# A planner's account of DMA speed in a selective-scan and feed-forward kernel: 220 or 300 KB per microsecond

## The reference

```python
proj = x @ W_in.T; u, gate = split(proj)              # 2 x 2048 channels
u = silu(causal_conv4(u) + conv_b)
dt, B, C = split(u @ Wx.T)                            # 64, 16, 16 columns, each rms-normed
delta = softplus(dt @ Wdt.T + dt_bias)
state = exp(delta * A) * state + delta * u * B        # a scan over 512 steps, 2048 channels x 16 states
y = (sum over the 16 states of state * C + u * D) * silu(gate)
x = layernorm(x + y @ W_out.T)
x = layernorm(x + x @ W.T + b + the low-rank product that a router picks for the row)
```

## Time and profile before

| | |
|---|---|
| runs | 2258.07, 2259.97, 2263.01 us; median 2259.97 |
| span of the profiled execution, first to last instruction | 2257.2 us |
| its own time | not listed apart from the runs; the median run is 2.8 us above this span |
| TensorE, VectorE, ScalarE, GpSimd busy | 91%, 88%, 66%, 81% of the span |
| TensorE clock granted, mean | 0.964 of full speed |
| DMA | 354.84 MB, mean 157 GB/s |

### The profile page before, as it was taken

The page is one execution under the profiler, slowest core; times in us unless marked ns, Lnnn a source line. Parts: engine busy times, 40 slices in busy tenths (PEclk is TensorE's granted clock), DMA queues, the critical chain, the costliest instruction groups (busy, mean ns, idle before and its releaser), DMA issues. The chain is left out here.

```text
span 2257.2 us, 30761 instructions
## 1 busy us (share of the span) xinstructions
PE 2063.3 (91%) x10528; PEld 1562.5 (69%) x10528; DVE 1986.4 (88%) x2398; ACT 1486.3 (66%) x2198; POOL 1824.8 (81%) x786
## 2 busy tenths in 40 slices
PE   8989789889999799799998997989999998897998
PEld 6867577778565478687875555867875556785677
DVE  4447779999999999899999999999999999999943
ACT  4478658787666677666886657676786667756531
POOL 4279899998898889768799997979788998698840
PEclk9989899999999999999999998999999999998999
DMA  4466566665333447655463432475463337443340
GB/s 157 138 223 235 204 221 219 203 205 179 92 118 86 126 132 239 209 193 182 158 199 95 111 96 96 147 264 171 143 203 101 110 96 233 148 144 132 101 143 38
DMA packets 168764, 354.84 MB, mean 157 GB/s; under 512 B 18656, under 2 KB 45408, under 8 KB 168608
## 3 DMA queue, kind: packets, MB, share of 16 engines
q1 hardware_dynamic: 168608, 352.87, 48.6%
HBM read 283.96 MB, written 68.85 MB: 156 GB/s over the span
## 5 line engine op out<-in xcount | busy, mean ns | idle before, releaser
L1563 POOL TENSOR_TENSOR drive<-delta_u,b_bcast 128x2048 f32<-128x2048 f32 (+1 forms) x257 | 1172.5, 4564 | 129.1 <-PE state_t L933 120.6
L1115 DVE TENSOR_TENSOR_SCAN drive<-decay,drive 128x512 f32<-128x512 f32 x1024 | 1190.5, 1203 | 62.0 <-POOL drive L1563 37.9
L1355 ACT ACTIVATE decay<-delta,a_sb 128x512 f32<-128x512 f32 x1024 | 694.7, 688 | 377.9 <-DVE drive L1115 374.6
L933 PEld LDWEIGHTS state_t<-identity,drive 128*128 128x128 f32 x4096 | 492.0, 146 | 311.1 <-DVE drive L1115 141.8
L933 PE MATMUL state_t<-identity,drive 128*128 128x128 f32 x4096 | 591.1, 284 | 119.8 <-DVE drive L1115 95.1
L1123 DVE SCALAR_TENSOR_TENSOR y_acc<-state_t,c_rows,y_acc 128x512 f32<-128x512 f32 x727 | 515.3, 734 | 54.3 <-PE state_t L933 51.7
L964 PE MATMUL bank<-cols_high,w_split 128*128 128x512 f32 (+1 forms) x1240 | 524.4, 423 | 26.6 <-POOL w_split L1588 11.8
L966 PE MATMUL bank<-cols_high,w_split 128*128 128x512 f32 (+1 forms) x1240 | 491.8, 397 | 0.0
L965 PE MATMUL bank<-cols_low,w_split 128*128 128x512 f32 (+1 forms) x1240 | 489.6, 395 | 0.0
L987 PE MATMUL bank<-channels,w_raw 128*128 128x512 f32 x896 | 420.2, 596 | 2.3 <-DVE rows L1177 2.0
L1568 POOL TENSOR_TENSOR y_acc<-y_acc,scaled 128x512 f32<-128x512 f32 x233 | 300.1, 1288 | 102.2 <-ACT scaled L1375 101.9
(11 more groups left out here) (204 smaller groups left out, 1451.8 us busy)
## 6 DMA issues: line engine op xcount, KB each, us to landing
w_split<-w_split SPq DMA_DIRECT2D x272, 512.0 KB, 4.0
b_bcast<-b_rows SPq DMA_DIRECT2D x256, 256.0 KB, 3.4
w_raw<-in_w_out SPq DMA_DIRECT2D x112, 256.0 KB, 3.0
w_raw<-in_w_in SPq DMA_DIRECT2D x96, 256.0 KB, 4.1
gates<-scratch SPq DMA_DIRECT2D x64, 256.0 KB, 3.7
scratch<-gates SPq DMA_DIRECT2D x64, 256.0 KB, 4.7
rows<-in_x_rows SPq DMA_DIRECT2D x4, 2048.0 KB, 8.2
out<-rows SPq DMA_DIRECT2D x16, 512.0 KB, 4.8
```

The lines of the kernel that those rows point to most:

```text
L933: last = engine.transpose(bank[0:tile.shape[1], i * P:(i + 1) * P], tile, identity[:, :])
L1115: engine.tensor_tensor_scan(state, decay[(GT * s + t) % DECAYS][:, :], state, 0.0, ALU.mult, ALU.add).then_inc(signal["scan"])
L1355: engine.activation(decay[i % DECAYS][:, :], delta[:, g % 2, t, :], ACT.Exp, scale=a_sb[:, j, n:n + 1]).then_inc(signal["decay"])
L1563: engine.tensor_tensor(drive[key % DRIVES][:, tiles, :], du[:, tiles, :], row, ALU.mult).then_inc(signal[stage])
```

## The change

The rate in the account of the planner becomes a constant of 300 KB per us instead of 220. A piece that lost against its rival is remembered, and isn't made ready later. A transposition lists all four scans of its unit as needed, and the stream waits for them in falling order.

```diff
+    RATE = 300.0
@@ arrange
-        now, dma, ends, finished, wanted, table = 0.0, 0.0, [], 0, len(self.pieces), None
+        now, dma, ends, finished, wanted, table, dropped = 0.0, 0.0, [], 0, len(self.pieces), None, set()
...
                         wanted -= pieces
+                        dropped.add(lost)
...
-                        dma = max(dma, at[e]) + piece["kb"] / 220.0
+                        dma = max(dma, at[e]) + piece["kb"] / self.RATE
...
-                    if left[follower] == 0:
+                    if left[follower] == 0 and follower not in dropped:
@@ make_plan
-            put("PE", i + 4 - TURN_FIRST, 0.45, "turn", (s, tt), [("scan", (s, GT - 1)), ...
+            put("PE", i + 4 - TURN_FIRST, 0.45, "turn", (s, tt), [*[("scan", (s, t)) for t in range(GT)], ...
@@ block.tensor
-                    e.wait_ge(*done("scan", (s, GT - 1)))
+                    for t in reversed(range(GT)):
+                        e.wait_ge(*done("scan", (s, t)))
```

More of the change, by code:

```diff
@@ L578, in make_plan @@
             turned = [("turn", (s, tt)), ("ssm_norm", b)]
-            put("PE", i + 4 - TURN_FIRST, 0.45, "turn", (s, tt), [("scan", (s, GT - 1)), *([] if i else [("ssm_norm", 0)])] + (
+            put("PE", i + 4 - TURN_FIRST, 0.45, "turn", (s, tt), [*[("scan", (s, t)) for t in range(GT)], *([] if i else [("ssm_norm", 0)])] + (
                 [turn_read(*divmod(i - TURNED, TT))] if i >= TURNED else []))
```

## The result

The changed kernel takes 2232.57 us (median of 4 runs, 2230.95 to 2236.01) against 2259.73 us before (median of 4 runs too): a ratio of 0.9877, 95% interval 0.9863 to 0.9891. That is 27 us less. The prediction had the direction and the place of the largest part; the size, 8 us, was less than a third of it.

A forecast was written before the change was run, and what follows sets the result against it. The prediction took GpSimd to bound the kernel up to 300 us, then VectorE with TensorE close behind. Its terms, -6 - 5 + 3 = -8 us, gave a time of 2252 us, forecast range 2238 to 2255, outer ends 2232 and 2278.

The forecast's parts named there:

- (c): On all engines, the rate from 220 to 300 KB per us reorders the work: the whole change, -8 us.
- I take 6, half of either row: From 141.9 to 300 us, 6 us gained of GpSimd's 12.5 us waiting for rounded weights.
- nothing to do with the order: Before the first scan, VectorE's 13.6 us wait for the very first product was held independent of the order.
- rarely takes all: From 141.9 to 300 us, rearranging in-order streams was said to rarely take all of the 12.5 us.
- up to some 8 us behind: From 150 to 225 us, loads in the old account were said to lag by up to some 8 us.
- The later stretches: Dense stretches between 300 and 1950 us: 5 us gained of VectorE's 33.7 us idle.
- The cost of early landings: Input weights from 110 to 525 us, believed earlier: 20 us of lateness, nearly all on ScalarE, 3 us let through.
- Steps (a) and (b): The guard against making lost alternatives, and transposes waiting for all four scans of a unit: 0 us each.
- What was to be seen: Signs: 960 additions, product waits below 30 us and weight waits below 8 up to 300, later scan idle within 10.
- No additional wait on TensorE: Sign over the whole kernel: TensorE's stream was to get no additional wait.
- Rival 1: Whole kernel: the order changes but the time doesn't, 2260 us (2255.5 to 2264.5); chance 0.19.
- Rival 2: From 110 to 525 us, landings taken too early make ScalarE's stream wait: slower, +14 us, 2274; chance 0.22.

The follow-up runs named there:

- e9: The changed kernel with rate 300 only while the account's clock is under 300 us, 220 after: 2247.66 us, 0.9941.
- e10: The changed kernel with rate 220 while the account's clock is under 300 us, 300 after: 2256.19 us, 0.9981.
- experiments 2 and 3: Queue at 300 with landings of 220 (2226.97 us) and the reverse (2271.46 us); then the changed kernel at rates from 200 to no limit.
- e1: The kernel before with the rate 300 alone, no guard, transposes as before: 2233.13 us, 0.9877.
- e2: The changed kernel with its rate put back to 220, guard and waits for four scans alone: 2262.31 us, 0.9999.

## Why the prediction was wrong in size

*The term that was mis-sized* is the first of (c), "I take 6, half of either row", for the first stretch. It is 16.7 us there, and 6.3 more before the first scan. Two judgements failed. The bound was set at the 12.5 us that GpSimd waits for weights; the right bound was all of GpSimd's idle time beside the same work, 17.6 us, and the new order recovered 16.8 of it. And the longest wait for a product, 13.6 us, was set aside as having "nothing to do with the order". It had: 6 us of it were the order of four instructions on GpSimd (the two timelines above). That the account had the row of B late, and so let the second half pass, is what its own times say (landing at 137.07 us, the first half done at 129.96); that the early rate does it is shown (lead 5.9 us in e9, 0.0 in e10). The issue of the row at 130.46 us beside a product at 139.46 could have been read in the trace of before.

That a rearrangement "rarely takes all" was a habit and rested on no row. The arithmetic of the backlog (18,240 KB take 82.9 us of the account and 75 of the chip) was right in kind, and experiments 2 and 3 confirm it: half a microsecond on single landings does nothing that can be told, the drain of the queue nearly all. But its "up to some 8 us behind" is a mean and not a maximum: in the account of before, transfers issued from 140 to 300 us of the account stand 7.8 us behind others on the mean and 14.7 at most.

*The later stretches*, -5: the scans from 64 to 1023 lost 4.1 us net (lead 23.0 to 18.9), with swings of 14.3 and 12.3 us inside, and the tail, which I hadn't looked at, gave 9.1. The sum -6 - 5 + 3 = -8 is in truth -6.3 - 16.7 + 4.1 - 9.1 = -28.0. The tail's share was visible as a place with dense DMAs (its first 35 us move 220 GB/s) that I passed over since no scans run there. But dense DMAs alone are not enough for a gain: from 1490 to 1520 us, where the chip moved 291 GB/s, transfers stand 8.9 us behind on the mean in the account of before, yet the lead is 27.7 us at scan 656 (1434 us of the kernel before) and 27.3 at scan 720 (1573). VectorE was busy 28.76 of the 30 us there, so that there was little to win.

*The cost of early landings*, +3 of 20 us: ScalarE's waits for input weights went from 11.3 to 13.8 us, so this much held. Two waits that the prediction took at nothing came beside it: TensorE's 6.9 us for split weights, where before there was none, and GpSimd's for rows of B, from 2.5 to 5.3 us. The lead fell by 2.0 us across the longest of them (scans 896 to 914), so the size of this term may well be right; the 12.3 us lost up to scan 928 read for the most part as the four normalizations on ScalarE, another order and not a late landing. The row of 4.0 us that the prediction calls the 512 KB load mixes some 80 stores of pairs (L853) with the loads (L864).

*Steps (a) and (b)* were right, at 0 us each (e1, e2). *What was to be seen*: VectorE's wait for products from 141.9 to 300 fell below 30 us (15.5), GpSimd's for rounded weights below 8 (2.7), the additions make 960, and VectorE's idle time in the scans from 300 us on is 71.4 us after 69.5. "No additional wait on TensorE" did not hold (6.9 us). Against the prediction: it called itself wrong if a gain arises from 525 to 825 us, where few DMAs run; the lead grows there by some 5 us (scans 192 to 352: 16.1 to 20.9). e9, which has the old rate there, swings by as much (its lead is 12.3 us at scan 256 and 19.0 at 320), so that this is within what reordering does.

*Rival 1* (no effect) had 0.19 on the ground that transfers wait for buffers and not for the DMA engines. That row is about the chip. What decides is whether they wait in the account. *Rival 2* is real, but far away: it needs landings of 2.35 us for 512 KB where the chip has 4.0 to 4.8. The fit of the Trainium skill's "DMA: Bandwidth & Descriptors" (Anatomy of one DMA) lies between, at 3.2 us by my estimate; the trace does not agree with it (3.8 to 4.8 us), and no run here gave the account that landing.

## What to carry to other kernels

When an order is made by an account of the machine, compare the account's throughput with the densest stretch of the trace, not with the mean: 225 GB/s looked ample against a mean of 157, and was short of the 249 to 291 of its dense stretches. And these are no upper bound of what the chip moves: the new order had 338 GB/s from 880 to 910 us, where the old one had 276. A backlog that exists only in the account cost 69 us over a fifth of the rate (250 to 200), while landings believed half a microsecond too early or too late cost nothing that stands out of the scatter. From 1490 to 1520 us, where VectorE had hardly any idle time, the backlog cost nothing that can be seen. Size such a gain by the idle time of the engine that bounds the stretch, then measure neighbours of the chosen value: here two settings 3% apart differ by 22 us, so a single run of one setting would have told little of the cause.

## What was not expected of the hardware

The denser order moved 257 GB/s over 158 us where 226 had been, without the landings suffering much: the median of the input weights over the kernel went from 4.1 to 4.4 us, that of 512 KB from 4.0 to 4.2. From 880 to 910 us it moved 338 GB/s, more than the 307 of its own account and the 276 of the same 30 us before. The stage view of the changed kernel:

```profile
141.90:300.00 158.10, 140.67 (x732) 115.10 (x733) 127.23 (x138) 126.75 (x189) 155.41 (x75) 0.94 0.73 257
...
880.00:910.00 30.00, 27.43 (x154) 22.08 (x153) 29.29 (x35) 20.25 (x31) 28.95 (x15) 1.00 0.95 338
```

TensorE's busy time is not the same for the same 10528 instructions: 2063.3 us before, 2057.4 after, and 2078.6 at the rate 200. The mean granted clock of these executions is 0.964, 0.965 and 0.953. At the rate 200:

```profile
PE 2078.6 (90%) x10528; PEld 1573.6 (68%) x10528; DVE 1988.2 (86%) x2398; ACT 1485.0 (64%) x2196; POOL 1825.2 (79%) x786
```

The granted clock has two levels here, 1.2 and 2.4 GHz. One stretch of the kernel before at the lower one (0.50 of full speed):

```profile
122.50:130.00 7.50, 5.20 (x14) 2.89 (x14) 1.45 (x5) 4.47 (x7) 2.13 (x2) 0.50 0.72 268
```

Ahead of it TensorE had been idle for 2.07 us up to 113.07 and for 4.04 us up to 122.53. The clock is still low just after: the 128x512 product with input weights that starts at 131.46 us takes 0.63 us, where the same one at 104.58, at full clock, took 0.39. The slow order at the rate 200 keeps TensorE idle for 225 us in all (2303.4 - 2078.6) against 172 in the changed kernel (2229.2 - 2057.4), and its same matmuls are busy 21 us longer (2078.6 - 2057.4). That the additional gaps are what lowered the clock fits these rows; no run tests it alone.
